# The end of a routed list: a tile that reaches back to the last row, and empty rows written at fixed places

## The reference, cut to what matters

```python
x = x + xattn(layernorm(x), ctx)          # x: (8, 256, 256); 16 heads of 16
gate = softmax(flat_x @ w_gate.T)         # flat_x = layernorm(x), 2048 tokens of 256
topk_scores, topk_idx = top_k(gate, 2)    # 8 experts
cw = (one_hot(topk_idx, 8) * topk_scores[..., None]).sum(axis=1)
h = gelu(einsum('td,edh->teh', flat_x, W1) + b1)     # 1024 hidden columns
y = einsum('teh,ehd->ted', h, W2) + b2
x = x + einsum('ted,te->td', y, cw)
```

## Time and profile before

| | us |
|---|---|
| median of 3 runs | 506.69 (506.08 to 507.53) |
| the profiled execution, device time | 508.38 |
| its span, first to last instruction | 507.0 |
| PE / PEld busy | 443.7 / 374.6 |
| DVE / ACT / POOL busy | 363.7 / 326.5 / 175.0 |

### The profile page before, as it was taken

One profiled execution on the slowest core, in us unless ns is written; L12 is line 12 of the kernel. 1 busy time (PEld: TensorE's weight loads), 2 busy tenths in 40 slices (PEclk: granted clock), 3 DMA queues, 4 the chain that ended last, 5 costly groups with the idle time before them and its releaser, 6 DMA issues.

```text
span 507.0 us, 10200 instructions
## 1 busy us (share of the span) xinstructions
PE 443.7 (88%) x3586; PEld 374.6 (74%) x3586; DVE 363.7 (72%) x803; ACT 326.5 (64%) x523; POOL 175.0 (35%) x220
## 2 busy tenths in 40 slices
PE   5798979998968986969989797999999999999892
PEld 3355656676756653558989797999889898898882
DVE  4556776777766874567879984987777879689651
ACT  2123775676645644749869674988686967869650
POOL 5146241372508437030554422242221422222213
PEclk9898999999989997898989899999999999999978
DMA  7693624324123114660576599698787796887702
GB/s 234 197 252 122 219 105 136 118 87 136 70 82 127 67 55 148 254 263 19 203 231 218 170 279 326 219 270 244 232 239 277 212 307 195 264 293 214 222 12 34
DMA packets 44624, 93.19 MB, mean 184 GB/s; under 512 B 6990, under 2 KB 30350, under 8 KB 38684
## 3 DMA queue, kind: packets, MB, share of 16 engines
q1 hardware_dynamic: 35340, 81.56, 47.7%
q0 software_dynamic: 7152, 9.46, 9.4%
q10 hardware_dynamic: 2080, 1.49, 1.0%
HBM read 63.10 MB, written 14.32 MB: 153 GB/s over the span
## 4 chain that ended last, share of the span: by engine, by line
PE 46%; DVE 15%; DMA 13%; ACT 10%; issue 10%; SPq 4%; POOL 1%; another core or an unknown queue 0%; ACTq 0%; DVEq 0%; POOLq 0%
DMA w_in<-in_W 8%; PE bank L1393 8%; PE S L1357 7%; PE bank L1460 6%; DVE nmax L951 5%; PE S L1492 5%; PE bank L1452 3%; ACT hf L1169 3%; PE bank L1527 3%; PE bank L1443 3%; PE S L1515 2%; PE bank L1435 2%; ACT W2p L1141 2%; ACT Q L1129 2%; DMA lists<-zero 2%
## 5 line engine op out<-in xcount | busy, mean ns | idle before, releaser
L582 POOL DMA_INDIRECT out<-y,slot x39 | 69.9, 1791 | 176.2 <-DVE y L859 102.0
L951 DVE TENSOR_REDUCE nmax<-S 128x4 f32<-128x1024 f32 x64 | 78.3, 1224 | 49.2 <-PE S L1492 49.1
L1357 PE MATMUL S<-xgT,Q 128*128 128x256 f32 x512 | 97.3, 289 | 1.6 <-DVE xgT L825 1.4
L1265 ACT ACTIVATE prob<-S 128x1024 f32<-128x1024 f32 x64 | 65.8, 1028 | 33.4 <-PE S L1515 32.3
L1357 PEld LDWEIGHTS S<-xgT,Q 128*128 128x128 f32 x512 | 80.0, 192 | 2.7 <-issue 2.7
L1393 PE MATMUL bank<-W2p,hp 128*128 128x256 f32 x528 | 71.3, 294 | 5.5 <-DVE y L855 5.5
L802 DVE TENSOR_TENSOR K<-w_in,Q 128x1024 fp32r<-128x1024 f32 x46 | 55.9, 1223 | 24.6 <-ACT Q L1129 23.5
L1169 ACT ACTIVATE hf<-S,b1c 128x256 f32<-128x256 f32 x128 | 53.1, 467 | 30.8 <-PE S L1357 26.9
L1357 PE MATMUL S<-xgT,K 128*128 128x256 f32 x256 | 72.7, 284 | 0.0
L1393 PEld LDWEIGHTS bank<-W2p,hp 128*128 128x128 f32 x528 | 67.7, 200 | 5.8 <-issue 5.8
L841 DVE TENSOR_TENSOR hp<-hf,hp 128x512 fp32r<-128x512 f32 x64 | 44.1, 689 | 19.4 <-ACT hp L1189 19.3
(11 more groups left out here) (211 smaller groups left out, 818.7 us busy)
## 6 DMA issues: line engine op xcount, KB each, us to landing
w_in<-in_W SPq DMA_DIRECT2D x46, 1024.0 KB
K<-flat_k SPq DMA_DIRECT2D x24, 256.0 KB, 2.4
Q<-flat_q SPq DMA_DIRECT2D x24, 256.0 KB
xg<-lists SPq DMA_DIRECT2D x16, 265.0 KB
b_in<-in_b SPq DMA_DIRECT2D x23, 128.0 KB
lists<-zero SPq DMA_DIRECT2D x9, 265.0 KB
cin<-in_ctxT SPq DMA_DIRECT2D x8, 256.0 KB, 3.9
xin<-in_x SPq DMA_DIRECT2D x8, 256.0 KB, 4.1
```

The lines of the kernel that those rows point to most:

```text
L582: st_y[i % 4].after(pool.indirect_dma_start(out=out, out_offset=bass.IndirectOffsetOnAxis(ap=slot[i % 4][:, t:t + 1], axis=0), in_=y[i % 2 ...
L951: max_done.after(dve.tensor_reduce(nmax[n % 4][:, :, :, m].rearrange("p t r -> p r t"), S1[:].rearrange("p r (t k) -> p r t k", t=TT), AX. ...
L1265: exp_done.after(act.activation(prob[s % 4][:].rearrange("p r t l -> p (r t l)"), S2[:].rearrange("p r l -> p (r l)"), ACT.Exp, scale=SCALE))
L1357: ins = pe.matmul(h_bank[pair][:, u, 0:n], W1p[k][a][:, kc, m * P:(m + 1) * P], xgT[k][c][:, kc, 0:n], start=(j == 0), stop=(j == len(term ...
```

## The change

Each expert's list now starts 256 rows further on, and the 256 rows ahead of it are the empty ones. A last tile that would reach past the end of its list is moved back so that its last row is the list's last row; in a list shorter than a tile it reaches back into the empty rows. A tile that was moved back shares rows with the tile before it, and those rows must count once: `shifts` holds, for each late tile, up to which of its rows the gate is made zero, and `rows_low` applies it when it copies the gates. The places of the empty rows are now constants, so they are written during the attention, one block of 265 KB every four steps from step 14 to step 46, nine in all (eight lists and the block behind them that unused tiles point to, which was written at step 12 before). `empty_ends` and `zrow` are gone, the small write of the b1 rows goes from step 30 to 31, and `assign` has more operations and three more steps for the late tiles.

```diff
@@ sp_tile, tile 6
             if i:
                 ld_w1[k].after(sp.dma_start(w1_in[k], w1))
-            if i == EARLY - 1:
-                empty_ends()
             if i >= 2:
                 sp.wait_ge(w2_lo.sem, 2 * (i - 1))
...
-        def empty_ends():
-            sp.wait_ge(zrow_done.sem, 1)
-            for f in range(NE):
-                z = sp.value_load(zrow[0:1, f:f + 1], min_val=f * REGION, max_val=f * REGION + REGION - TS)
-                st_zero.after(sp.dma_start(lists[bass.ds(z, TS), :].rearrange("(t p) e -> p t e", p=P), zero[:]))
@@ sp_attention
-                st_zero.after(sp.dma_start(lists[NE * REGION:, :].rearrange("(t p) e -> p t e", p=P), zero[:]))
+            def empty_list(e):
+                st_zero.after(sp.dma_start(lists[e * REGION:e * REGION + TS, :].rearrange("(t p) e -> p t e", p=P),
+                                           zero[:]))
...
-                if s == 30:
+                if s >= 14 and (s - 14) % 4 == 0 and (s - 14) // 4 <= NE:
+                    empty_list((s - 14) // 4)
+                if s == 31:
                     sp.wait_ge(b1_lo.sem, 1)
@@ constants
-                pool_const.after(pool.memset(base[:, e:e + 1], float(e * REGION)))
+                pool_const.after(pool.memset(base[:, e:e + 1], float(e * REGION + TS)))
@@ assign, for the late tiles
+                if ended:
+                    done(dve.tensor_tensor(risen[k][:, 0:n], beyond[k][:, 0:n], over(rise_end[:], shape), ALU.mult))
                 done(dve.scalar_tensor_tensor(picked[k][:, 0:n], number[:, 0:n], float(rows_each), picked[k][:, 0:n],
                                               ALU.mult, ALU.add))
                 yield
                 ready()
+                if ended:
+                    c = slice(start - EARLY, start - EARLY + n)
+                    done(dve.tensor_reduce(room[k][:], risen[k][:, 0:n], AX.X, ALU.add))
+                    done(dve.tensor_scalar(picked[k][:, 0:n], picked[k][:, 0:n], step_[k][:, 0:1], float(NE * REGION),
+                                           ALU.add, ALU.min))
+                    yield
+                    ready()
+                    done(dve.scalar_tensor_tensor(room[k][:], room[k][:], last_from[k][:, 0:1], picked[k][:, 0:n], ALU.add,
+                                                  ALU.subtract))
+                    yield
+                    ready()
+                    done(dve.tensor_scalar(shifts[:, c], room[k][:], -1.0, float(TRASH), ALU.mult, ALU.add))
+                    yield
+                    ready()
+                    return dve.scalar_tensor_tensor(table[:, 0, start:start + n], room[k][:], 0.0, picked[k][:, 0:n],
+                                                    ALU.min, ALU.add)
@@ lists_of, stage 3
-            zrow_done.after(dve.tensor_tensor(zrow[:], counts, base[:], ALU.add))
+            done(dve.tensor_tensor(ends[:], counts, base[:], ALU.add))
...
+            done(dve.tensor_tensor(rise_end[:, 0:NE - 1], ends[:, 1:NE], ends[:, 0:NE - 1], ALU.subtract))
             yield
             ready()
+            done(dve.tensor_scalar(last_from[0][:], ends[:, 0:1], -float(TS), None, ALU.add))
+            done(dve.tensor_scalar(last_from[1][:], ends[:, 0:1], -float(P), None, ALU.add))
@@ rows_low
-            scale_done.after(dve.tensor_copy(scale[i % 4][:, 0:HT[i]], xg[k][:, 0:HT[i], bass.ds(e + (E + 1), 1)]
-                                             .rearrange("p t o -> p (t o)")))
+            gates_ = xg[k][:, 0:HT[i], bass.ds(e + (E + 1), 1)].rearrange("p t o -> p (t o)")
+            if i < EARLY:
+                scale_done.after(dve.tensor_copy(scale[i % 4][:, 0:HT[i]], gates_))
+            else:
+                scale_done.after(dve.scalar_tensor_tensor(scale[i % 4][:, 0:HT[i]], zero[:, 0:HT[i], E],
+                                                          shifts[:, c - EARLY:c - EARLY + 1], gates_, ALU.is_ge, ALU.mult))
```

More of the change, by code:

```diff
@@ L275, in build @@
         table = sb(top, "table", [P, 2, NTILE], I32)
-        zrow = sb(top, "zrow", [P, NE], I32)
+        shifts = sb(top, "shifts", [P, WHOLE + PARTS])
+        ends = sb(top, "ends", [P, NE])
+        rise_end = sb(top, "rise_end", [P, NE])
+        last_from = [sb(top, f"last_from{i}", [P, 1]) for i in range(2)]
+        room = [sb(top, f"room{i}", [P, n]) for i, n in enumerate((WHOLE, PARTS))]
         number = sb(top, "number", [P, WHOLE])
@@ L558, in pool_constants @@
             for e in range(NE):
[L559 to L560 removed]
+                pool_const.after(pool.memset(base[:, e:e + 1], float(e * REGION + TS)))
+                pool_const.after(pool.memset(base_far[:, e:e + 1], float(e * REGION + TS) + FAR))
             for i in range(3):
@@ L648, in list_constants @@
                     pool_r.after(pool.memset(rise[i][:, NE - 1:NE], float(NE * REGION)))
+                pool_r.after(pool.memset(rise_end[:, NE - 1:NE], 2.0 * NE * REGION))
             for s in range(START, LAST):
@@ L693, in prefix, with assign @@
                 yield
-            def assign(k, n, start, rows_each):
+            def assign(k, n, start, rows_each, ended=False):
                 shape = [P, n, NE]
@@ L790, in lists_of @@
             ready()
-            last = yield from assign(0, WHOLE, EARLY, TS)
+            last = yield from assign(0, WHOLE, EARLY, TS, ended=True)
             done(last)
-            last = yield from assign(1, PARTS, EARLY + WHOLE, P)
+            last = yield from assign(1, PARTS, EARLY + WHOLE, P, ended=True)
             table_done.after(last)
```

5 lines of the change are left out of this document (1 added, 4 removed).

## The result

| | before | after |
|---|---|---|
| median, us | 506.65 (502.85 to 514.69, 20 executions) | 503.06 (496.89 to 507.31, 20 executions) |
| mean, us | 507.39 | 502.85 |
| profiled execution: device time, span | 508.38, 507.0 | 503.12, 501.6 |
| PE, DVE busy | 443.7, 363.7 | 441.2, 367.2 |

The kernel is faster: the ratio is 0.9911, with a 95% interval of 0.9887 to 0.9936. That is a gain of 4.5 us by the ratio and by the means, of 3.6 by the medians; -2.46 was forecast. Each kernel's executions scatter with a standard deviation of 2.7 us, so a single profile shows a mechanism well and a size of a few us badly. The ratio compares the executions near each kernel's fastest, which is why it and the medians differ.

A forecast was written before the change was run, and what follows sets the result against it. TensorE was taken to bind, idling 2.84 us for tile 7's rows behind the writes of empty rows. -2.84 + 0.38 = -2.46 us from the median 506.69 gave 504.2 us, range 502.4 to 506.6.

The forecast's parts named there:

- The stall goes whole: TensorE's wait for tile 7's rows, behind the writes of empty rows, was to vanish entirely: -2.84 us.
- Everything behind tile 7: The loop of late tiles was said to run at its own pace from wherever it is entered; no term in the sum.
- The term of -2.84 us: TensorE's idle time from 309.73 to 312.57 before turning tile 7's rows, counted as saved in full.
- rival 3: More comes back than the idle time, half clock behind a stall also being saved: 502.7 us, chance 0.15.
- Signs of being wrong: Waits for rows or weights before tile 5 or 7, step 48 later, or W1's late load under 2.46 us earlier.
- List work ahead of the stall, +0.38 us: Four list operations added on VectorE ahead of the stall at 286, all on the path: +0.38 us.
- The 0.71: Upper bound, in us, for the four list operations ahead of the stall at 286, each costing its full duration.
- List work behind it, 0 us: Added VectorE work behind the stall at 286, 1.65 us, covered by 2.60 us before tile 5, leaving 0.95: 0 us.
- rival 1: The stall comes back elsewhere, at tile 5's rows, tile 7's W1 or by half clock: 505.6, up to 507; chance 0.22.
- Blocks in the attention, 0 us: Eight new blocks at steps 14 to 46, each 0.51 us of SyncE, fit into free queue time: 0 us.
- rival 2: Blocks in the attention are not free, delaying loads and stackings behind them: 508.3 us at full cost, chance 0.08.
- The gate in late tiles, 0 us: In each late tile VectorE compares and multiplies a gate instead of copying it, with the same number of operations: 0 us.

The follow-up runs named there:

- third turn: Both kernels run again unchanged on one chip: the kernel before 1.0039, mean 507.32 us; the changed kernel 0.9891, mean 503.46 us.

## Where the prediction was right, and why its size was off

*The stall goes whole.* Right, and by the steps given; filling the old lists early, with nothing else changed at that place, takes it away as well (11.85 us from tile 6 to 7). Less the 2.42 us by which this execution is late, tile 6's W2 was issued at 297.76 (forecast near 298) and tile 7's rows at 300.34 (forecast 300.9); they were there in time. One step was right for a reason that I hadn't weighed: I took the freed issue time as what matters, but late writes without any wait make the same stall (3.02 us), so the traffic ahead of the rows is enough for it.

*Everything behind tile 7 was put at nothing, and this is the step that failed.* The prediction said of the loop of late tiles that it "runs at its own pace from wherever it is entered", and so the sum has no term for it or for the end. That holds up to tile 14 (78.21 us before, 78.14 after). Behind it the two profiles differ by 4.73 us: 1.09 in tiles 14 to 22 and 3.64 at the end. In the profiles of the experiments as well:

| kernels | tiles 14 to 22, us | tile 22 to the end, us |
|---|---|---|
| before, three turns and with blocks added | 82.39, 81.85, 82.66, 82.15 | 33.83, 29.57, 32.64, 33.71 |
| before, with products in the wait | 80.71 | 30.97 |
| changed, three turns | 81.30, 81.38, 81.84 | 30.19, 28.96, 29.11 |
| old lists filled early, twice | 81.13, 81.20 | 29.91, 28.71 |
| late writes put back, five times | 80.91, 80.81, 80.86, 81.17, 81.45 | 29.55, 29.27, 31.84, 31.22, 29.11 |

So putting the late writes back doesn't bring most of the longer late stretch back. By the times of many executions what was put at nothing is 1.7 ± 0.8 us; its cause stays open (both in the last paragraph).

*The term of -2.84 us came from one profile and left the clock out.* In one profile each, kernels with the stall showed 2.84, 3.85, 4.08 and 3.20 (the kernel before, and with blocks added), 2.90, 3.00, 3.02, 3.11 and 2.81 (late writes put back). Tile 6 to 7 fell from 14.85, 15.84, 16.09 and 15.20 us to 11.82 to 11.85, that is by 3.0 to 4.3 us, 3.7 in the mean. And behind five of these nine stalls the granted clock fell, and the next tiles took 1.5 us more (tiles 7 to 14 in 79.6 to 79.7 us instead of 78.1 to 78.2). That was rival 3, to which I gave 0.15; it is no rival but happens in part of the executions, and belongs into the term with its frequency. Yet this can't be all of the gap. Over many executions the stall, with the clock behind it, is worth 2.8 ± 0.6 us (below), which is the size that the term had; side by side with a kernel without it, it was 4.3 and 4.8 us on one chip, 2.9 and (old lists, six executions) nothing on another, and 1.9 on a third. A sum of -3.7 - 0.75 + 0.33 = -4.1 us from the profiles would come near the measured -4.5, but it would put into the stall what the executions don't find there.

*Signs of being wrong.* Two of those named came up in the profile after, and both by the late start of this execution. Step 48 is reached 1.10 us later than before; in the third turn of both kernels it is reached 0.02 us earlier. And W1's load in the pair of late tiles is issued at 382.83 instead of 383.51, 0.68 us earlier and not 2.46; from tile 7's turning to it it is 70.86 us, and 70.94 before.

*List work ahead of the stall, +0.38 us.* Right: from the split of the hidden rows to the emptying of tile 2's outputs it took VectorE 13.48 us before and 13.81 after, +0.33. The price of an operation was confirmed by ten more of them, 0.20 each, but the half clock behind the stall grew with them, which neither the term nor its bounds had. The 0.71 of every operation at its full duration, which the Trainium skill's page "VectorE: DVE Perf Modes", section "The DRAIN you can't avoid", gives without its exception, was not paid in the profile.

*List work behind it, 0 us.* Right, and closer than forecast: 1.98 us instead of 1.65 (one operation, `picked`, took 0.55), with 0.63 of cover left instead of 0.95. Ten operations more there turn into a wait of 0.78 us, so rival 1 lay 0.6 us away. It did not come.

*Blocks in the attention, 0 us.* Right: against rival 2 stand the one distance of 1.05 us that the steps 12 to 44 keep, and the blocks alone in the kernel before, 0.9975.

*The gate in late tiles, 0 us.* Right: tiles 7 to 14 take 78.14 us against 78.21.

*What is not settled.* The stall put back five times gave 0.9951, 0.9972, 0.9862, 1.0061 and 0.9969. By means against the kernel before on the same chip, weighted by their errors, that is -2.3 ± 0.4 us; the kernels without the stall (the changed one three times, the old lists filled early twice) give -5.1 ± 0.4; the kernel before again, and with blocks added, -0.6 ± 0.7. The difference of the first two, 2.8 ± 0.6 us, is the stall's, shown by putting it back. The other step, from -0.6 to -2.3, is 1.7 ± 0.8 us, hardly clear of chance, and what makes it no run isolates. The kernels with the stall put back lack the late writes at places read at run time into the lists; but the kernel before with products in the wait has them, and it was 3.5 us faster with a short late stretch. So the late writes are not shown to be the cause. The profiles differ in the pairs of late tiles and at the end. There TensorE waits for W1's low terms, before and after:

```profile
480.86 0.47 PE L1367 MATMUL S<-b1r,ones 2*128 2x512 f32 x1 [1.61 <-DVE K L802]
```

```profile
481.00:486.00 5.00, 5.00 (x13) 3.06 (x14) 4.08 (x6) 3.26 (x6) 0.00 (x0) 0.62 0.00 0
```

```profile
478.54 0.46 PE L1392 MATMUL S<-b1r,ones 2*128 2x512 f32 x1 [1.04 <-DVE K L823]
```

```profile
481.00:486.00 5.00, 4.88 (x35) 4.37 (x35) 4.02 (x6) 2.93 (x5) 1.56 (x1) 1.00 0.00 0
```

The first two are of the kernel before, timeline and window: a wait of 1.61 us, and the clock at 0.62 behind it. The other two are of the changed kernel: 1.04 us, and the full clock. In profiles of the kernel before this last wait was 1.61 and 1.66 (third turn), 1.72 with blocks added, each time with half clock behind it, but below 0.5 in the second turn; in all other kernels it was 1.26 or less. The three profiles with the wait are of executions of 508.38, 514.45 and 508.05 us, the one without it is of the fastest of its twelve, 503.84. So the wait tends to go with the kernel before, isn't fixed to it, and may go with long executions instead; why W1 is later there was not found.

## What to carry to other kernels

A stall's price read from one profile is one draw: before it goes into a sum, profile the kernel again, and see how often half clock follows it. The same holds for a stretch that goes into the sum as nothing: compare it tile by tile in a second pair of profiles before and after, and put the stall back to see what hangs on it. Here, with writes ahead of a load in a queue, the transfers held the load as much as the wait did, so it was the writes that had to move, to where the DMA engines and the queue were idle. And work laid ahead of a stall cost its full delay, 0.20 us for a small VectorE operation, while behind it the same work was free up to the cover.

## What the runs showed of the hardware

- Half clock followed TensorE's idle times unevenly. Behind the stall ahead of tile 7 it followed 3.00, 3.02, 3.11, 3.85 and 4.08 us, and didn't follow 2.81, 2.84, 2.90 and 3.20. The stall of 3.02 to 3.19 us ahead of tile 2's outputs had slow products behind it in every profile but one: in the kernel before, third turn, 24 products behind 3.04 us took 3.11. In the late tiles it followed waits as short as 1.34 and 1.61 us, and there it didn't follow 1.28. The row of 1.34 us is of the kernel with the last list's work behind the units, with its windows:

```profile
409.19 0.47 PE L1395 MATMUL S<-b1r,ones 2*128 2x512 f32 x1 [1.34 <-DVE K L823]
```

```profile
404.00:409.00 5.00, 3.85 (x33) 3.64 (x31) 3.80 (x8) 4.94 (x10) 3.55 (x2) 1.00 0.97 274
409.00:414.00 5.00, 4.82 (x12) 2.99 (x13) 4.29 (x6) 4.43 (x7) 0.78 (x1) 0.65 0.51 106
```

  TensorE was busy for 3.85 of the 5 us ahead of it. Such a busy time doesn't tell the cases apart either: with the old lists and the late writes put back (first time) it was 3.75 of 5 us ahead of a wait of 1.25 us, and the clock stayed at 1.00. From tile 16's turning to tile 17's it took 13.42 us, and 10.56 in the changed kernel. The Trainium skill, page "TensorE: Matmul & The Clock Gate", section "The HAM clock gate", explains half rate by how busy the engine was recently; the busy times read here neither show that nor speak against it.
- One kernel on one chip scatters by 0.9 to 4.4 us (standard deviation, of 5 to 35 executions) from execution to execution, and the same kernel differs by 9 us between chips (500.0 to 508.8 us in the mean for the kernel before), so only runs of one chip can be compared.
- Tile 7's rows, 265 KB, landed in 4.52 us when they were issued after the empty rows had landed; issued at 300.28, behind 2.1 MB of writes and 1 MB of W2 on the same queue, they took up to 11.5 us.
